# One launch of a two-stage graph network on 12,500 nodes and 200,000 edges: the first layer's edge stage joined with the count build, extra tiles one by one

## The chip, the core and the metric

The kernel runs on one NeuronCore of one Trainium2 chip. The core has five engines with queues of their own: TensorE (PE in the profile, its weight loads PEld), VectorE (DVE), ScalarE (ACT), GpSimd (POOL) and SyncE (SP). They share the on-chip memories and meet only at semaphores. The metric is the device time of one launch in microseconds (us); lower is better.

## What is computed

Three graph convolutions on the normalised input, and one message layer with edge features. Cut to what matters:

```python
loop = arange(N); s = concat([src, loop]); d = concat([dst, loop])      # every node also has itself
deg = segment_sum(1, d); dinv = rsqrt(deg)
norm = dinv[s] * dinv[d]
h = relu(layernorm(x))
for W, b in ((W1, b1), (W2, b2), (W3, b3)):                             # GCN layers 0, 1, 2
    h = segment_sum((h @ W)[s] * norm[:, None], d) + b                  # relu between layers
x = x + h
h = relu(layernorm(x))
filt = edge_attr_50 @ W_rad.T + b_rad
m = segment_sum((h @ W_pre.T + b_pre)[src] * filt, dst)
out = x + silu(m @ W_post.T + b_post)
```

There are 12,500 nodes with 64 features and 200,000 edges. The edges are sorted by destination `dst`, and the destinations are skewed: low nodes have many incoming edges, high nodes few. `src` is random. The dtype is float32.

## The kernel before

Nodes are cut into 98 windows of 128. Edges are cut into 196 blocks of 8 tiles of 128, and 4 blocks make a round. The first 50 windows of destinations (the head, 6400 nodes) are handled in another way than the rest (the tail):

- **Head, count build.** From the edges the kernel builds, once, the matrix of edge counts, source node by head destination. It goes by groups of 8 destinations: 800 groups, 16 to a window. For a group, DVE makes one one-hot of the source's row (`tile_hots`, L635) for its 2 main tiles of edges, and for each tile one one-hot of (source window, destination in the group), 784 wide (`joint_hot`, L859). PE multiplies them into PSUM (`joint_tile`, L1181, 2 matmuls of 392 columns a tile). A group whose edges lie in more than 2 tiles has extra tiles; they are made in sets of `EXTRA` = 2 tiles, two sets in flight. After two groups PE runs one closing matmul (L1215), and ACT turns the counts of both into fp8 in one go (L552). After a window, SP writes it to the HBM tensor `counts` (L396). The loop runs over 200 steps of 4 groups (`SETS`), and DVE may be 4 groups ahead of PE. DVE and PE read the tile numbers into registers at the start of a step (L887, L888, L1195).
- **Head, every GCN layer.** The counts of a window come back from HBM (L418), PE multiplies all 98 source windows of counts by the node features split in three bf16 parts (`dense_window`, L1098, 98 matmuls of 192 columns), and DVE adds the result to `node` (`take_dense`, L688, L692).
- **Tail, every GCN layer.** For 15 rounds of 4 blocks, POOL gathers the source rows of a block from the HBM tensor `table` (8 indirect DMAs, L500). DVE makes one-hots of the destinations (`one_hot`, L629) and splits the rows into three bf16 parts (`split_rows`, L646 to L653), PE multiplies (`product_split`, L1085, L1087), and DVE adds the sum to `sumT` (`add_sum`, L661). In a layer's edge pass a tail block and a head window take turns (`dense_turn`).

The order is written out by hand in one program for each engine: degrees, then the count build, then a layernorm (L601) and for each layer a projection (PE transposes and multiplies, DVE scales in L950 and writes the three parts in L960 to L966, SP writes `table`), the edge pass and a collection (L1000 to L1006). Within a projection's loop, DVE makes the parts of a group of 7 windows right behind that group's scaling. The number of rounds and of head windows comes from a check at the end of the build (`mode`, L929): if the counts do not add up to the degrees, every layer takes all edges as tail. For these inputs the counts add up. `gate` (L733) clears the head's sums where they are not wanted. The message layer takes all 196 blocks as tail, in float32, with edge filters.

## Time and profile before

| | us |
|---|---|
| median of 3 runs | 6310.55 |
| lowest and highest | 6275.51, 6314.47 |
| the profiled execution | 6314.64 |
| its span | 6312.8 |

| engine | busy us | share of the span |
|---|---|---|
| PE | 4668.7 | 74% |
| DVE | 3220.4 | 51% |
| POOL | 2908.4 | 46% |
| ACT | 856.6 | 14% |

Stages of the span, read from the times at which their lines first and last run: degrees and tables to 381 us, count build 381 to 1768, layernorm and projection 0 to 1886, edge pass 0 to 2539, collection 0 and projection 1 to 2668, edge pass 1 to 3303, the same again for layer 2 to 4068, collection, layernorm and projection to 4275, the message layer's edges to 6230, closing to 6312. An engine's busy share is an average over stages with different limits, so each stage is read by itself. Idle time in brackets stands before the instruction, with what ended it; "issue" means that the profile shows nothing that the engine waited for.

### The profile page before, as it was taken

Reading aid. Unit: us, or ns where it says so; the run is one execution under the profiler, and the core shown is the slowest. Engines: PE = TensorE matmul, PEld = TensorE weight load, DVE = VectorE, ACT = ScalarE, POOL = GpSimd, SP = SyncE. Lnnn points to the kernel's source line nnn. Section 1 sums busy time; section 2 is a strip of 40 time slices with the busy share of each in tenths; the row PEclk is TensorE's granted clock in tenths of the full one; section 3 lists DMA queues with packets and bytes.
Section 4 is the critical chain, followed back from the end, with each engine's and each line's share of the span. In section 5 each row is a group of like instructions: output and inputs, shape, how many; then the busy total and the mean of one; then the engine's idle time right before and its main releaser. Section 6 shows DMA issues by size and latency. Waiting matters only on the chain.

```text
span 6312.8 us, 113587 instructions
## 1 busy us (share of the span) xinstructions
PE 4668.7 (74%) x32080; PEld 3572.4 (57%) x32081; DVE 3220.4 (51%) x8761; ACT 856.6 (14%) x1382; POOL 2908.4 (46%) x3078
## 2 busy tenths in 40 slices
PE   6967676666659997799968999666666666666665
PEld 4732222222248885688847888455555555555555
DVE  6789998777764444644446444452222222222225
ACT  0002345555520000200001000010000000000002
POOL 0000000000007667177763766507777777777772
PEclk9999999999959997599976999656666666666665
DMA  1000011111114553155522555202222222222221
GB/s 32 0 0 41 41 61 61 71 71 71 71 60 160 167 168 94 53 172 167 174 65 82 167 170 173 64 24 47 46 47 47 47 46 47 47 46 47 47 46 34
DMA packets 165567, 484.92 MB, mean 77 GB/s; under 512 B 68364, under 2 KB 81740, under 8 KB 139924
## 3 DMA queue, kind: packets, MB, share of 16 engines
q1 hardware_dynamic: 69268, 385.60, 16.9%
q0 software_dynamic: 96256, 98.76, 8.3%
q8 instruction: 25, 0.41, 0.0%
q14 instruction: 18, 0.15, 0.0%
HBM read 387.82 MB, written 96.33 MB: 77 GB/s over the span
## 4 chain that ended last, share of the span: by engine, by line
PE 38%; POOL 25%; issue 16%; DVE 12%; DVEq 7%; DMA 1%; SPq 0%; POOLq 0%; ACT 0%; ACTq 0%
POOL rows_flat L500 25%; PE ps L1098 20%; DVE node L859 6%; PE ps L1155 5%; PE ps L1070 4%; PE ps L1087 4%; PE ps L1085 3%; DVE hot L635 2%; PE ps L1181 1%; DVEq L859 1%; DVEq L888 1%; PE ps L1056 1%; DVEq L887 1%; DVEq L635 1%; DVEq L903 1%
## 5 line engine op out<-in xcount | busy, mean ns | idle before, releaser
L500 POOL DMA_INDIRECT rows_flat<-table,row_stage x3008 | 2870.4, 954 | 1549.2 <-issue 1308.7
L1078 PE MATMUL ps<-hot,msg_flat 128*64 128x160 f32 x3136 | 807.9, 445 | 728.8 <-DVE msg_flat L722 728.8
L1181 PE MATMUL ps<-node,hot 128*128 128x392 f16 x4268 | 914.6, 342 | 489.6 <-DVE node L859 473.1
L1098 PE MATMUL ps<-wide,ring 128*128 128x192 bf16 x14700 | 1244.9, 247 | 0.0
L1098 PEld LDWEIGHTS ps<-wide,ring 128*128 128x128 fp8e4 x14700 | 1210.5, 98 | 13.0
L1078 PEld LDWEIGHTS ps<-hot,msg_flat 128*64 128x64 f32 x3136 | 649.9, 215 | 843.4 <-issue 711.4
L859 DVE TENSOR_SCALAR node<-rows_flat,wide 128x784 f16<-128x784 f16 x2134 | 928.8, 477 | 0.0
L1181 PEld LDWEIGHTS ps<-node,hot 128*128 128x128 f16 x4268 | 355.4, 100 | 940.2 <-issue 639.7
L484 POOL TENSOR_TENSOR found<-found,found_ring 128x8 f32<-128x8 f32 x50 | 24.7, 494 | 1698.9 <-ACT ring L552 1698.9
L629 DVE TENSOR_SCALAR hot<-iota,dst_rel 128x160 f32<-128x160 f32 (+1 forms) x3008 | 639.7, 291 | 265.2 <-issue 262.7
L552 ACT ACTIVATE ring<-ps 128x1568 fp8e4<-128x1568 f32 x400 | 590.8, 1477 | 763.6 <-PE ps L1215 763.3
L722 DVE TENSOR_TENSOR msg_flat<-rows_flat,ps 128x512 f32<-128x512 f32 x196 | 134.7, 687 | 1009.5 <-DMA rows_flat<-table,row_stage 1009.3
L565 ACT COPY row_stage<-row_i 128x8 int32 x376 | 74.0, 197 | 3741.7 <-DVE sumT L661 3737.6
L635 DVE TENSOR_TENSOR hot<-onehot_more,wide 128x256 f16<-128x256 f16 x1067 | 378.3, 355 | 229.9 <-issue 122.2
L1118 PEld LDWEIGHTS ps<-w_rad,ring 51*128 51x128 f32 x3136 | 431.0, 217 | 58.4 <-issue 58.4
L1118 PE MATMUL ps<-w_rad,ring 51*128 51x64 f32 x3136 | 459.8, 305 | 0.0
L688 DVE TENSOR_REDUCE dense_sum<-ps 128x64 f32<-128x192 f32 x150 | 53.7, 358 | 655.8 <-PE ps L1098 655.8
L661 DVE TENSOR_TENSOR sumT<-sumT,ps 64x160 f32 (+1 forms) x376 | 119.4, 318 | 486.0 <-issue 379.3
L1155 PE MATMUL ps<-hot 128*128 128x98 bf16 x1568 | 296.5, 360 | 50.5 <-DVE hot L635 50.5
L1155 PEld LDWEIGHTS ps<-hot 128*128 128x128 bf16 x1568 | 210.5, 147 | 135.7 <-issue 50.2
L1085 PE MATMUL ps<-hot 128*128 128x160 bf16 x720 | 182.6, 254 | 124.0 <-DVE hot L653 124.0
L635 DVE TENSOR_TENSOR hot<-onehot_more,ring 128x1024 bf16<-128x1024 bf16 (+1 forms) x392 | 229.0, 626 | 67.1 <-PE ps L1155 67.1
(146 smaller groups left out, 2945.6 us busy)
## 6 DMA issues: line engine op xcount, KB each, us to landing
ring<-counts SPq DMA_DIRECT2D x150, 1568.0 KB
counts<-ring SPq DMA_DIRECT2D x50, 1568.0 KB, 5.1
rows_flat<-table,row_stage POOLq DMA_INDIRECT x3008
ring<-in_radial SPq DMA_DIRECT2D x196, 200.0 KB
table<-node SPq DMA_DIRECT2D x56, 224.0 KB, 1.9
out<-node SPq DMA_DIRECT2D x13, 224.0 KB
ring<-in_dst SPq DMA_DIRECT2D x1, 784.0 KB
ring<-in_src SPq DMA_DIRECT2D x1, 784.0 KB
```

The lines of the kernel that those rows point to most:

```text
L500: nc.gpsimd.indirect_dma_start(out=rows[:, j, k * D:(k + 1) * D], out_offset=None, in_=table[:, :], in_offset=bass.IndirectOffsetOnAxis(ap ...
L552: nc.scalar.activation(to, of, ACT.Identity, scale=float(UNIT), saturate=True, accum_out=found_ring[:, h, t:t + 1]).then_inc(sub_copied, 1)
L629: one = nc.vector.tensor_scalar(to[:, k, :], columns, rel[:, bass.ds(tile0 + k, 1)], None, ALU.is_equal)
L635: return nc.vector.tensor_tensor(to, columns, of.unsqueeze(1).to_broadcast(to.shape), ALU.is_equal)
L859: return nc.vector.tensor_scalar(to, iota_joint, sub_start[:, bass.ds(sub, 1)], joint_of[:, bass.ds(t, 1)], ALU.add, ALU.is_equal)
L1070: z = nc.tensor.matmul(ps_z[:, h, i * D:(i + 1) * D], stage_fn[0:n, h, i * P:(i + 1) * P], w, start=True, stop=True)
L1078: s = nc.tensor.matmul(to, of, mats[:, k, :], start=(k == 0), stop=(k == BLOCK_TILES - 1))
L1085: nc.tensor.matmul(to, split_upper[j % 2][:, k, :], mat, start=(k == 0), stop=False, skip_group_check=True)
L1098: d = nc.tensor.matmul(ps_dense[:, h, :], count_ring[:, h, q, :], parts[:, q, :], start=(q == 0), stop=(q == WINDOWS - 1))
L1118: f = nc.tensor.matmul(ps_filt[:, j % 2, k * D:(k + 1) * D], radial_sb[:, j, k * P:(k + 1) * P], w_rad[:, :], start=True, stop=True)
L1155: d = nc.tensor.matmul(ps_deg, rem_hot[:, a, :, k], win_hot[:, a, :, k], start=(first and k == 0), stop=(last and k == BLOCK_TILES - 1))
L1181: m = nc.tensor.matmul(to[:, c, :], sources[:, :, k], joint[k][:, c * (JOINT // 2):(c + 1) * (JOINT // 2)], start=first, stop=True, skip_g ...
```

## The change

The first layer's layernorm, projection and table write now stand ahead of the count build. The build loop becomes `build_and_first_layer`: 25 iterations (pairs of windows) of 4 quarters. A quarter builds 8 groups (`subs` twice), then PE multiplies half a finished window of counts (`dense_part`, 49 matmuls, straight from the ring, without the way through HBM), and, in the first 15 iterations, a tail block is split, multiplied and added. Which rounds are tail is known before the build now (`tail_known`); the check comes afterwards, and if it fails the first layer is done again (`REDO`), which does not happen for these inputs. The counts are still written to HBM for layers 1 and 2.

With it come: `EXTRA` = 1, extra tiles made one by one in two buffers; the second main tile of a group is multiplied last, behind the extra tiles, and the closing matmul is gone; ACT converts one group at a time, 784 values instead of 1568, and the two PSUM buffers hold one group each instead of two; the found counts are added by DVE instead of POOL; POOL's gathers wait for `slot_free`; bases of tail blocks are clamped to the head's end and put back (`unclamp`) ahead of the message layer; the `gate` multiply is gone; and in every GCN projection the three bf16 parts are made in a second loop behind the whole first one (and behind clearing `sumT`), instead of within it.

The diff, cut to its core:

```diff
-EXTRA = 2
+EXTRA = 1
-        ps_count = [ps[:, 4 * a:4 * a + 4, 0:JOINT // 2] for a in range(2)]
+        ps_count = [ps[:, 4 + 2 * a:6 + 2 * a, 0:JOINT // 2] for a in range(2)]
@@ scalar
+            def evict(i, h, t):
+                act.wait_ge(main_used, i * (2 * TURNS) + (h * TURNS + t + 1 + SETS))
+                of = ps_count[t % 2].rearrange("p a (q d) -> p a q d", d=SUB)
+                nc.scalar.activation(to, of, ACT.Identity, scale=float(UNIT), saturate=True,
+                                     accum_out=found_ring[:, h, t:t + 1]).then_inc(sub_copied, 1)
@@ vector
-                dve.wait_ge(slot_free, at.turn(at.rounds, SLOTS))
-                nc.vector.tensor_scalar(sumT[:, 0:HEAD * P], sumT[:, 0:HEAD * P], gate[:, 0:1], None, ALU.mult)
+            def project(p):
+                with dve.Fori(0, GROUPS // 2) as g2:
+                    for h in range(2):
+                        ...
+                            nc.vector.tensor_tensor(mine, z, over_features(dinv[:, groups(g2 * 2 + h)]),
+                                                    ALU.mult).then_inc(z_used, 1)
+                if p:
+                    then(nc.vector.memset(sumT[:, :], 0.0))
+                settle()
+                if p < GCN_LAYERS:
+                    dve.wait_ge(z_used, (PROJECT(p) + 1) * GROUPS + 2)
+                    with dve.Fori(0, GROUPS) as g:
+                        ...
+                        nc.vector.tensor_copy(part[0], mine).then_inc(step, 1)
+                        nc.vector.tensor_tensor(tmp[:, :, :], mine, part[0], ALU.subtract).then_inc(step, 1)
+                        nc.vector.tensor_copy(part[1], tmp[:, :, :]).then_inc(step, 1)
+                        nc.vector.tensor_tensor(part[2], tmp[:, :, :], part[1], ALU.subtract).then_inc(step, 1)
+                    dve.drain().then_inc(parts_ready, 1)
+            def build_and_first_layer():
+                dve.wait_ge(table_written, 16 * GROUPS)
+                at = Pass(dve, FUSED)
+                with dve.Fori(0, PAIRS) as i:
+                    for j in range(SLOTS):
+                        h = j // 2
+                        with dve.Fori(0, P // SUB // SETS // 2) as q:
+                            subs(i * (2 * P // SUB // SETS) + j * (P // SUB // SETS // 2) + q)
+                        if j == 0:
+                            with dve.If(i > 0):
+                                take_dense(0, last, 0)
+                                keep_found(last, 1)
+                                with dve.If(last < at.rounds):
+                                    add_sum(at, last, SLOTS - 1, P)
+                        if j == 2:
+                            with dve.If(i > 0):
+                                take_dense(0, earlier(i), 1)
+                            keep_found(i, 0)
+                        with dve.If(i < at.rounds):
+                            split_block(at, i, j)
+                            if j:
+                                add_sum(at, i, j - 1, P)
+                            add_more(at, i, j, ps_more_fused[j % 2])
+            layernorm(2)
+            project(0)
+            build_and_first_layer()
@@ tensor
+            def dense_part(i, h, part):
+                if part == 0:
+                    pe.wait_ge(sub_copied, i * (2 * TURNS) + ((h + 1) * TURNS + 2))
+                    pe.wait_ge(dense_taken, i * 2 + (h + 1))
+                for q in range(part * (WINDOWS // 2), (part + 1) * (WINDOWS // 2)):
+                    d = nc.tensor.matmul(ps_dense[:, h, :], count_ring[:, h, q, :], parts[:, q, :],
+                                         start=(q == 0), stop=(q == WINDOWS - 1))
-                    if a % 2 == 0:
-                        pe.wait_ge(sub_copied, s4 * (SETS // 2) + (a // 2 + 1))
+                    pe.wait_ge(sub_copied, s4 * SETS + (a + 1))
-                    for k in range(MAIN):
-                        m = joint_tile(to, src_main[a], joint_main[a], k, k == 0)
-                    m.then_inc(main_used, 1)
+                    for k in range(MAIN - 1):
+                        joint_tile(to, src_main[a], joint_main[a], k, k == 0)
                     ...
-                    if a % 2:
-                        nc.tensor.matmul(to[:, 1, 0:1], zeros16[:, :], zeros16[:, 0:1],
-                                         start=False, stop=True, skip_group_check=True).then_inc(built, 1)
+                    joint_tile(to, src_main[a], joint_main[a], MAIN - 1, False).then_inc(main_used, 1)
+            def build_and_first_layer():
+                with pe.Fori(0, PAIRS) as i:
+                    for j in range(SLOTS):
+                        with pe.Fori(0, P // SUB // SETS // 2) as q:
+                            subs(i * (2 * P // SUB // SETS) + j * (P // SUB // SETS // 2) + q)
+                        if j < 2:
+                            with pe.If(i > 0):
+                                dense_part(earlier(i), 1, j)
+                        else:
+                            dense_part(i, 0, j - 2)
+                        with pe.If(i < at.rounds):
+                            split_block(at, i, j, ps_more_fused[j % 2])
```

Two places in the order of the instructions. In the first, a GCN layer's projection on DVE before: each group's scaling (L950, from PSUM into `node`) is followed by the instructions that write its parts into `wide`.

```order
L950 TENSOR_TENSOR node<-ps,dinv 128x448
L960 ISA
L960 REGISTER_ALU
L960 COPY wide<-node 128x7x64
```

And the same place in the change (layer 0), where L998 is the scaling, and L1009 the head of the second loop, which holds the four instructions on the parts (L1017 to L1023).

```order
L998 TENSOR_TENSOR node<-ps,dinv 128x448
L993 REGISTER_ALU
L993 COMPARE_AND_BRANCH
L1009 UNCONDITIONAL_BRANCH
L1009 ISA
L1017 ISA
L1017 REGISTER_ALU
L1017 COPY wide<-node 128x7x64
```

The parts have moved behind the end of the scaling loop. The second place is PE at the end of a step of 4 groups. Before, the group's matmuls (`node` holds the joint one-hots, `hot` those of the source) end with the closing matmul, and the next thing is the loop's own branch:

```order
L1181 MATMUL ps<-node,hot 128x392 x4
L1190 REGISTER_ALU
L1211 UNCONDITIONAL_BRANCH
L1215 MATMUL ps<-zeros 128x1
L1194 REGISTER_ALU
L1194 COMPARE_AND_BRANCH
```

In the change (`sumT` and `stage_fn` hold the one-hots now), after the extra tile's two matmuls the second main tile's two follow, then the inner loop's branch (L1390), half a window of counts (L1354) and the tail block (L1238, L1240, repeated 8 times):

```order
L1343 MATMUL ps<-sumT,stage_fn 128x392 x2
L1364 REGISTER_ALU
L1382 UNCONDITIONAL_BRANCH
L1343 MATMUL ps<-sumT,stage_fn 128x392 x2
L1390 REGISTER_ALU
L1390 COMPARE_AND_BRANCH
L1393 COMPARE_AND_BRANCH
L1350 ISA
L1351 ISA
L1354 MATMUL ps<-wide,ring 128x192 x49
L1393 UNCONDITIONAL_BRANCH
L1397 COMPARE_AND_BRANCH
```

So the work of the first layer's edge pass now stands in PE's queue between groups of the build. In the built program the outer loop of the build is 826 instructions long on DVE; the longest loop on DVE before is 286. On PE it is 1241, against 1057 before.

## Rows read from the trace of the kernel before

**Rows 1.** Busy time by stage; columns are named in the first line.

```profile
core 0: us, PE busy (x) PEld busy (x) DVE busy (x) ACT busy (x) POOL busy (x), PEclk, DMA share, GB/s
381.00:1768.00 1387.00, 923.85 (x4668) 395.35 (x4666) 1155.39 (x3197) 626.71 (x800) 24.52 (x49) 0.97 0.14 57
1768.00:1886.00 118.00, 67.01 (x294) 57.63 (x294) 83.41 (x114) 20.48 (x34) 0.66 (x3) 0.50 0.11 41
1886.00:2539.00 653.00, 593.14 (x5860) 501.95 (x5860) 269.41 (x881) 11.05 (x56) 459.29 (x480) 0.92 0.46 147
```

**Rows 2.** Timeline of DVE in the build: start, length, instruction, idle before.

```profile
1352.62 0.29 DVE L635 TENSOR_TENSOR hot<-onehot_more,wide 128x256 f16<-128x256 f16 x1 [0.94 <-issue]
...
1358.00 0.29 DVE L635 TENSOR_TENSOR hot<-onehot_more,wide 128x256 f16<-128x256 f16 x1 [1.05 <-PE ps L1181]
```

**Rows 3.** Timeline of DVE in the build, behind a window's write.

```profile
1387.27 0.43 DVE L635 TENSOR_TENSOR hot<-onehot_more,wide 128x256 f16<-128x256 f16 x1 [2.36 <-issue]
```

**Rows 4.** Timeline of DVE in the build, extra sets of one group.

```profile
390.93 0.29 DVE L635 TENSOR_TENSOR hot<-onehot_more,wide 128x256 f16<-128x256 f16 x1 [0.17 <-issue]
...
393.17 0.29 DVE L635 TENSOR_TENSOR hot<-onehot_more,wide 128x256 f16<-128x256 f16 x1 [0.18 <-issue]
```

**Rows 5.** Timeline of PE's weight loads in the build, two groups.

```profile
1354.95 0.46 PEld L1181 LDWEIGHTS ps<-node,hot 128*128 128x128 f16 x4 [0.68 <-issue]
...
1355.94 0.46 PEld L1181 LDWEIGHTS ps<-node,hot 128*128 128x128 f16 x4 [0.20 <-issue]
```

**Rows 6.** Timeline of ACT in the build, one conversion of two groups.

```profile
1352.80 1.48 ACT L552 ACTIVATE ring<-ps 128x1568 fp8e4<-128x1568 f32 x1 [0.54 <-PE ps L1215]
1354.18 0.19 ACT L552 ACTIVATION_READ_ACCUMULATOR ring<-ps 128x1 f32 x1
```

**Rows 7.** Timeline of edge pass 0, one turn on DVE, then PE's window of counts.

```profile
2004.93 1.49 DVE L629 TENSOR_SCALAR hot<-iota,dst_rel 128x160 bf16<-128x160 bf16 x8 [0.76 <-issue]
...
2007.98 0.69 DVE L653 TENSOR_TENSOR hot<-hot 128x512 bf16<-128x512 f32 x1
2013.26 0.36 DVE L688 TENSOR_REDUCE dense_sum<-ps 128x64 f32<-128x192 f32 x1 [4.58 <-PE ps L1098]
2013.78 0.23 DVE L692 SCALAR_TENSOR_TENSOR node<-dense_sum,node 128x64 f32 x1 [0.17 <-DVE dense_sum L688]
2014.79 0.32 DVE L661 TENSOR_TENSOR sumT<-sumT,ps 128x160 f32 x1 [0.78 <-issue]
2015.87 0.80 DVE L629 TENSOR_SCALAR hot<-iota,dst_rel 128x160 bf16<-128x160 bf16 x4 [0.76 <-issue]
2004.96 8.26 PE L1098 MATMUL ps<-wide,ring 128*128 128x192 bf16 x98
```

**Rows 8.** Groups of instructions, the page's and edge pass 0's: count | busy, mean.

```profile
L859 DVE TENSOR_SCALAR node<-rows_flat,wide 128x784 f16<-128x784 f16 x2134 | 928.8, 477 | 0.0
L500 POOL DMA_INDIRECT rows_flat<-table,row_stage x480 | 459.3, 957 | 292.3 <-issue 256.1 <-ACT row_stage L565 36.2
```

**Rows 9.** Timeline of DVE at the end of projections 0 and 1.

```profile
1882.10 0.62 DVE L950 TENSOR_TENSOR node<-ps,dinv 128x448 f32 x1
...
2641.14 0.62 DVE L950 TENSOR_TENSOR node<-ps,dinv 128x448 f32 x1
2641.98 0.62 DVE L960 CAST wide<-node  x1 [0.23 <-DVE node L950]
...
2644.17 0.62 DVE L966 TENSOR_TENSOR wide<-tmp,wide 128x448 f32 x1
2647.39 10.64 DVE L971 MEMSET sumT<- 128x12704 f32 x1 [2.60 <-issue]
```

**Rows 10.** Timeline of DVE at the end of edge pass 0.

```profile
2538.77 3.55 DVE L733 TENSOR_SCALAR sumT<-sumT,gate 128x6400 f32<-128x6400 f32 x1 [0.86 <-DVE sumT L661]
```

**Rows 11.** The page's DMA queues: packets, MB, share of 16 engines.

```profile
q8 instruction: 25, 0.41, 0.0%
q14 instruction: 18, 0.15, 0.0%
```

511 lines of the change are left out of this document (317 added, 194 removed).

## Prediction

> **What bounds the kernel now.** I read first the busy time by stage [rows 1]. The build takes 1387 us and edge pass 0 takes 653. In the build DVE is busy for 1155 us and PE for 924; in the edge pass PE is busy for 593 and DVE for only 269. The two stages lean on different engines, so joining them looks promising. The question is what is left of it when the idle time of DVE in the build turns out not to be free.
>
> The timeline of DVE in the build answers that. A step of 4 groups without extra tiles takes 1358.00 - 1352.62 = 5.38 us [rows 2], steadily, step after step. The idle 0.94 to 1.05 us ahead of it is the reading of two sets of registers and the loop's branch. The second row puts it down to PE, but the length of a step does not change with that label, and PE's groups wait a little for DVE (the 0.20 and 0.68 us in [rows 5]): I read it as DVE's own queue. So 200 x 5.38 = 1076 us of the build are DVE's, idle time included. Once per window, when its counts go out to HBM, a step is longer: DVE idles 2.36 us where otherwise it idles about 1 [rows 3], so some 1.2 us a window, 60 in all. The rest, 1387 - 1076 - 60 = 251 us, are the extra sets: the page counts 2134 one-hots of 784, 1600 are those of the main tiles, so 267 sets of two tiles [rows 8]. That is 0.94 us a set; in a long run of them two sets take 393.17 - 390.93 = 2.24 us [rows 4], 1.12 a set.
>
> PE is not far behind. From one group to the next where it hardly waits it takes 1355.94 - 1354.95 = 0.99 us [rows 5], though its matmuls are four; the rest is its queue's branches. In the edge pass a turn (a tail block and a window of counts) takes 2015.87 - 2004.93 = 10.94 us, of which the window is 8.26, all on PE [rows 7].
>
> **The build loop after the change, by quarters.** A quarter is two steps, half a window of counts and, in 60 of the 100 quarters, a tail block.
>
> DVE, in a quarter with a block: two steps, 10.76. The long read, 1.2 for two quarters, 0.6. One-hots and split from 2004.93 to 2008.67, 3.74 us; from the end of the counts' addition (2014.01) to the next one-hot (2015.87) lie 1.86 us with the block's own addition and its register reads [rows 7]; together 5.6. Taking a window, 0.36 + 0.23 and the gap between, 0.75 for two quarters, 0.4. Adding the found counts, two more conditions and an inner loop's start: about 0.6, an estimate from the 0.76 us that such reads and branches leave idle [rows 7]. Sum 18.0.
>
> PE, in the same quarter: the matmuls of 8 groups at 0.99 would be 7.9, plus the loop's end and read twice, about 1 us each as on DVE, so 9.9. But now the second main tile comes behind both branches, one PSUM buffer holds one group, and group n+2 may start only when ACT has converted group n. ACT's conversion of two groups is 1.48 + 0.19 [rows 6]; that of one lies between half of the first, 0.74, plus 0.19, and the whole. I take 1.0. A group of about 1.2 us from its first weight load to its last matmul, its conversion, and two hand-overs of about 0.1 make 2.4 us for two groups, 1.2 a group: 8 groups in 9.7 to 10.7, I take 10.4. Half a window is 4.1, a block's products are what is left of the turn, 10.94 - 8.26 = 2.7, conditions 0.3 [rows 7]. Sum 17.5. DVE may be 4 groups ahead, and while it splits a block PE multiplies counts, so the two overlap: the quarter is the longer sum and a little, 18.2 us. 60 of them: 1092.
>
> Without a block DVE needs 18.0 - 5.6 = 12.4 and PE 17.5 - 2.7 = 14.8: PE sets the pace, 15.0 us. 40 of them: 600.
>
> Extra tiles: by the input's destinations there are 388 one by one, where there were 267 sets. Each costs between half a set, 0.47, and a whole one, 0.94; its one-hots are half of a set's, its waits and registers a whole set's. I take 0.64, 250 us, so that edit alone is worth nothing against 251: fewer one-hots (1988 for 2134) and more turns. The last window's products stand behind the loop, 8.3. The joined loop is then 1092 + 600 + 250 + 8 = **1950 us**. From both sides: with 17.3 and 13.8 a quarter and 0.5 a tile it is 1792; with 19.8, 16.8 and 0.9 it is 2217.
>
> **The hidden part: gathers.** POOL gathers a block in 8 instructions that are 0.957 us each [rows 8], with about 0.3 between them. That is some 10 us, and a block has a quarter of 18 us; a block's slot is free three quarters ahead. So the gathers lie under DVE's work, and would up to 1.8 times their length. Here DVE was 269 of 653 us busy [rows 1]; in the loop it is busy nearly always. The Trainium skill, page "SBUF — State Buffer", section on the shared port pair, says that DVE in its fast two-port modes locks GpSimd out of it, and that descriptors of GpSimd's own DMAs wait. That speaks against joining the gathers with DVE's busiest stage. With the rows' cover of 1.8 times it changes no term of mine.
>
> **What moves around it.** Before, layernorm and projection 0 end with the last scaling at 1882.10 + 0.62 [rows 9], 115 us behind the build's end; they stand ahead of the build now at the same price. But the parts follow in a loop of their own. One group's parts run from 2641.98 to 2644.17 + 0.62, 2.8 us [rows 9], 3.1 with the loop: 14 groups are 43 us in which PE waits for `parts_ready`, where before only the last group's 3 us stood there. For layer 0 that is 44 us (it covers the table's write and the first gathers). For layers 1 and 2 the parts come behind the 10.64 us of clearing, and the edge pass, bound by PE's windows, starts 40 us later each: +80. The cover that is gone is PE's time in the projection, which took 118 us with the layernorm for 67 of PE [rows 1]. The `gate` multiply goes, -3.6 in each of layers 1 and 2 [rows 10]. Clearing half of `sumT` before the build, -5. `unclamp`, about ten short DVE instructions, lies under the message layer's first gathers. The check after the loop, register reads and the empty `REDO` cost about what the old pass took to its collection: +1.
>
> **The sum.** Before, from the build's start at 381 to the last addition of edge pass 0 at 2538: 2157. After: -5 + 115 + 44 + 1950 + 1 = 2105, so -52. With +80 and -7 the change comes to **+21 us**. The profiled execution's span is 6312.8 (6314.6 with what lies around it) and the median 6310.55, 4 below: 6310.55 + 21 = 6332, I say **6335 us**.
>
> **The rivals.**
> 1. *The engines overlap better.* PE's groups run at 1.0 us and without blocks DVE sets the pace: quarters of 17.5 and 13 us, extra tiles at 0.55. The loop is 1050 + 520 + 213 + 8 = 1791, less than mine by 159. Halfway there, 1850, it gives 6235. For it speaks the 0.99 us of [rows 5]; against it that group n+2 waits for ACT. It decides below 1.05 us a group.
> 2. *A new wait: the conversion of single groups* (the one on the other side). One group in flight in each buffer ties PE to ACT and to itself. At 1.5 us a group, quarters are 20.2 with a block and 17.4 without: 1212 + 696 + 250 + 8 = 2166, +216, about 6550; at 1.35, 6440. ACT's 1.48 us for two groups speaks against the full price, and that PE's queue passes two branches in each group speaks for it. It decides above about 1.3.
> 3. *Code.* DVE's loop body is 826 instructions in the built program, three times its longest before; the page counts 25 and 18 code packets for the whole run [rows 11], so no loop before reads its code again. If this one does, and DVE waits as in the longest unexplained gap before a stage, 2.6 us [rows 9], once an iteration, it costs 15 x 2.6 = 39 us in the iterations with blocks; at each of five branches back, 195. Time 6375 to 6530. The Trainium skill, page "Runtime: NRT & Kernel Launch", section "Instruction fetch mechanics", has this as a rule: the instruction memory of an engine other than PE holds 512 instructions, and a taken branch out of it waits for a fetch. By that rule DVE's loop does not fit and all loops before do; what a wait costs here no row shows.
> 4. *It doesn't do what it says.* The first layer's work only lengthens each quarter, because PE's blocks come late every time: 10.8 + 4.1 + 2.7 + 3.7 = 21 us; loop 2100, 6485.
>
> **Chances.** Forecast 0.45 (own range 6270 to 6400); rival 1 0.20; rival 2 0.18; rival 3 0.12; rival 4 0.05. The range 6235 to 6480 leaves out the far end of rivals 1, 2 and 3. About 1%, 63 us, is what a measurement of this kernel can tell from no change. Below 6247 lies most of rival 1 and nothing else: 0.19. Above 6374 lie most of rivals 2 and 3, rival 4 and a tenth of the forecast: 0.36. The rest, 0.45, is within 1%.
>
> **What would show it.** In the profile after: in layers 1 and 2 the first product of counts stands 40 us further behind the last scaling than now; the loop from its first one-hot to the last window takes 1950 us; a quarter with a block takes 18 us and DVE is busy in it without waits for PE; one without takes 15 and DVE's one-hots of the source wait for PE's L1343; GpSimd is never named as what DVE waits for. DVE gaps of over 2 us at the outer loop's head, with many more code packets, would be rival 3. A busy ACT between PE's groups would be rival 2. Quarters far below 17 us, or a half clock in the loop (the granted clock is 0.97 in the build and 0.92 in the edge pass [rows 1], near the full 2.4 GHz), would prove my sum wrong.

## The result and the profile after

Over 20 timed runs of each, the changed kernel takes 6267.17 us (median, 6235.64 to 6323.17) and the kernel before 6314.46 (6275.51 to 6328.37). The ratio is 0.994, with a 95% interval of 0.9921 to 0.9959. So the change makes the kernel faster by 0.6%, surely but by less than 1%: the medians lie 47 us apart, the means 39. The forecast was 21 us slower. The measured time lies inside the stated range (6235 to 6480), but the change went the other way.

From the page of the profiled execution after (6264.8 us): the span, busy times, the code queues, and the two groups of one-hots of the joined loop.

```profile
span 6263.0 us, 114127 instructions
PE 4667.6 (75%) x31388; PEld 3424.1 (55%) x31389; DVE 3181.7 (51%) x8799; ACT 951.1 (15%) x2182; POOL 2930.3 (47%) x3027
q14 instruction: 217, 1.78, 0.1%
q8 instruction: 26, 0.43, 0.0%
L961 DVE TENSOR_SCALAR sumT<-stage_fn,sub_start,sumT 128x784 f16<-128x784 f16 x1988 | 891.5, 481 | 0.0
L508 POOL DMA_INDIRECT rows_flat<-table,row_stage x3008 | 2917.2, 970 | 2136.9 <-issue 1844.2
```

The busy times of PE, DVE and POOL hardly move; ACT's grows by 94 us. What moves besides is the idle time, and one queue: 217 packets of code, where [rows 11] has 18.

Busy time by stage after: layernorm and projection 0, parts 0, the joined loop (with blocks, and its last part without), projection 1 with its parts, edge pass 1, the scaling loop of projection 3.

```profile
core 0: us, PE busy (x) PEld busy (x) DVE busy (x) ACT busy (x) POOL busy (x), PEclk, DMA share, GB/s
372.00:485.00 113.00, 67.01 (x294) 57.64 (x294) 47.79 (x49) 20.15 (x33) 0.39 (x1) 0.50 0.07 27
485.00:531.00 46.00, 0.00 (x0) 0.00 (x0) 34.85 (x56) 0.00 (x0) 35.46 (x30) 0.50 0.12 24
531.00:1900.00 1369.00, 1085.76 (x6412) 521.13 (x6413) 1019.75 (x3055) 437.09 (x1003) 459.35 (x452) 0.91 0.14 46
1900.00:2480.00 580.00, 475.47 (x3426) 265.37 (x3425) 378.46 (x1055) 295.46 (x654) 0.41 (x1) 1.00 0.14 59
2533.00:2626.00 93.00, 32.68 (x267) 29.44 (x266) 54.24 (x71) 16.32 (x26) 35.65 (x32) 0.67 0.24 80
2626.00:3265.00 639.00, 591.66 (x5857) 501.14 (x5857) 268.82 (x879) 11.05 (x56) 429.12 (x448) 0.93 0.45 144
4158.00:4190.00 32.00, 32.00 (x265) 28.89 (x262) 7.95 (x13) 16.29 (x26) 0.00 (x0) 1.00 0.22 86
```

The two executions can be laid side by side at five marks (trace of before, trace of after, difference):

| from | to | before us | after us | difference |
|---|---|---|---|---|
| start | first scaling of projection 1 | 2590.2 | 2533.3 | -56.9 |
| first scaling 1 | first one-hot of edge pass 1 | 70.3 | 93.0 | +22.7 |
| edge pass 1 | first scaling 2 | 693.9 | 689.2 | -4.7 |
| first scaling 2 | first one-hot of edge pass 2 | 70.6 | 92.8 | +22.2 |
| edge pass 2 | first scaling 3 | 754.9 | 749.5 | -5.4 |
| first scaling 3 | first message one-hot | 75.7 | 52.7 | -23.0 |
| message layer | end | 2057.2 | 2052.5 | -4.7 |

The sum is -49.8, the difference of the spans. The joined loop, from its first one-hot at 531 to its last window's take at 2479, took 1948 us; 1950 was forecast. The reader is to see three things that the forecast did not have. The parts cost +22.7 and +22.2 where +40 was forecast. Projection 3, whose scaling loop was not changed, became 23 us shorter. And the joined loop is right as a sum of wrong terms, as the experiments show.

### The profile page after: what moved, and what is told of

Same layout as the page of the kernel before. It is cut to its first block, busy times and chain, and to the rows that moved or that the text cites. A ratio compares the mean times of both kernels' runs of the same rounds, so it can differ in the third digit from the quotient of the medians.

```text
span 6263.0 us, 114127 instructions
## 1 busy us (share of the span) xinstructions
PE 4667.6 (75%) x31388; PEld 3424.1 (55%) x31389; DVE 3181.7 (51%) x8799; ACT 951.1 (15%) x2182; POOL 2930.3 (47%) x3027
## 3 DMA queue, kind: packets, MB, share of 16 engines
q14 instruction: 217, 1.78, 0.1%
## 4 chain that ended last, share of the span: by engine, by line
PE 36%; POOL 25%; issue 18%; DVE 13%; DVEq 7%; DMA 1%; ACT 0%; SPq 0%; POOLq 0%; ACTq 0%
POOL rows_flat L508 25%; PE ps L1251 13%; PE ps L1343 5%; PE ps L1317 5%; PE ps L1223 4%; DVE sumT L961 4%; PE ps L1354 3%; PE ps L1240 3%; PE ps L1238 2%; DVE stage_fn L689 1%; PE ps L1209 1%; DVE hot L683 1%; DVEq L689 1%; DVEq L712 1%; DVE hot L1189 1%
## 5 line engine op out<-in xcount | busy, mean ns | idle before, releaser
L508 POOL DMA_INDIRECT rows_flat<-table,row_stage x3008 | 2917.2, 970 | 2136.9 <-issue 1844.2
L1343 PE MATMUL ps<-sumT,stage_fn 128*128 128x392 f16 x3976 | 980.4, 358 | 418.1 <-DVE sumT L961 234.4
L961 DVE TENSOR_SCALAR sumT<-stage_fn,sub_start,sumT 128x784 f16<-128x784 f16 x1988 | 891.5, 481 | 0.0
L1343 PEld LDWEIGHTS ps<-sumT,stage_fn 128*128 128x128 f16 x3976 | 287.8, 101 | 1086.6 <-issue 829.4
L585 ACT ACTIVATE ring<-ps 128x784 fp8e4<-128x784 f32 x800 | 658.5, 823 | 1255.5 <-PE ps L1343 1250.0
L689 DVE TENSOR_TENSOR stage_fn<-stage_fn,src_rem 128x256 f16<-128x256 f16 (+1 forms) x1188 | 393.7, 331 | 481.8 <-issue 289.4
L1354 PE MATMUL ps<-wide,ring 128*128 128x192 bf16 x4900 | 420.2, 246 | 6.0 <-ACT ring L585 3.6
L1354 PEld LDWEIGHTS ps<-wide,ring 128*128 128x128 fp8e4 x4900 | 402.3, 98 | 32.2 <-issue 28.2
L1238 PE MATMUL ps<-hot 128*128 128x160 bf16 x720 | 180.4, 251 | 173.9 <-DVE hot L707 173.8
```

Of the source, the lines that this page charges most:

```text
L508: nc.gpsimd.indirect_dma_start(out=rows[:, j, k * D:(k + 1) * D], out_offset=None, in_=table[:, :], in_offset=bass.IndirectOffsetOnAxis(ap ...
L585: nc.scalar.activation(to, of, ACT.Identity, scale=float(UNIT), saturate=True, accum_out=found_ring[:, h, t:t + 1]).then_inc(sub_copied, 1)
L689: return nc.vector.tensor_tensor(to, columns, of.unsqueeze(1).to_broadcast(to.shape), ALU.is_equal)
L961: return nc.vector.tensor_scalar(to, iota_joint, sub_start[:, bass.ds(sub, 1)], joint_of[:, bass.ds(t, 1)], ALU.add, ALU.is_equal)
L1238: nc.tensor.matmul(to, split_upper[j % 2][:, k, :], mat, start=(k == 0), stop=False, skip_group_check=True)
L1343: m = nc.tensor.matmul(to[:, c, :], sources[:, :, k], joint[k][:, c * (JOINT // 2):(c + 1) * (JOINT // 2)], start=first, stop=True, skip_g ...
```

## Experiment 1: is DVE's loop fetched again, and what does that cost?

DVE shows an idle stretch at the head of each iteration of the joined loop. Its timeline after, at two heads, 55.5 us apart:

```profile
2025.73 0.42 DVE L689 TENSOR_TENSOR stage_fn<-stage_fn,src_rem 128x256 f16<-128x256 f16 x1 [5.09 <-issue]
2081.27 0.29 DVE L689 TENSOR_TENSOR stage_fn<-stage_fn,src_rem 128x256 f16<-128x256 f16 x1 [5.35 <-issue]
```

A usual step has about 1 us there [rows 2]. In the trace's records the branch back (L1057) and the next instruction are 3.33 us apart in the median (2.73 to 3.91), 24 times, 80 us in all. Six kernels with loops of different length are compared. The cuts, in short (the first goes into all but the one with 554 instructions; the last into those with 554, 446 and 326):

```
-  If n > 1: Fori(0, n >> 1): extra tile in buffer 0, extra tile in buffer 1
-  If n & 1: extra tile in buffer 0
+  If n > 0: Fori(0, n): extra tile in the buffer that a register names (turn & 1)
...
-  add_more(at, i, j, ...)        # in the joined loop, on DVE, and more_products on PE
...
-  before each slot j:    Fori(0, 2) as q: subs(...)
+  before slots 0 and 2:  Fori(0, 4) as q: subs(...)
```

The lengths are those of DVE's loop body in the built program. The second cut leaves out the code for blocks that span more than 160 nodes, which these inputs never enter (510 and 326). A block's eight destination columns are also copied to a fixed place first, in the four kernels with the first cut.

> The kernel after with DVE's joined loop shortened from 826 to 630 instructions: one copy of an extra tile's code in place of three (its buffer chosen by a register), and a block's eight destination columns copied to a fixed place first. Same sums. Theory (the loop's code is fetched again at each branch back as long as it is too long): the gap of 3.4 us ahead of the first work of each iteration stays, an iteration without a block and without extra tiles stays at 55.3 us, code packets stay near 217. Rival (the gap is the loop's own branch and register reads, or grows with the length): it shrinks in the proportion 630 to 826, to 2.6 us, 54.5 us an iteration. An extra tile gets dearer by up to 0.2 us through the registers, so the whole loop is 1930 to 2030 us.

> As the kernel of 630 instructions, and without the code for spans of over 160 nodes in the joined loop on DVE and PE (these inputs never enter it): 510 instructions. Theory: the loop fits, the gap of 3.4 us at each of the 25 iterations falls under 1 us, an iteration without a block goes from 55.3 to about 52, code packets fall from 217 to near 18, and the whole is 85 us (1.4%) faster than with 630, of which some 5 are the skipped conditions. Rival (the gap has nothing to do with length): the gap stays at 3.4 us and the whole moves by under 10 us.

> The kernel after with one edit: the steps of the count build stand twice in the joined loop instead of four times (four steps in a row ahead of slots 0 and 2, none ahead of 1 and 3). DVE's loop body falls from 826 to 554 instructions. From the runs so far: with bodies of 630 and 510 the gap at the branch back was still 3.3 us an iteration and 7 and 6 packets of code came for each. Theory (the loop must fit whole, with what is fetched ahead of need): at 554 the gap is still 3.3 us, packets near 6 an iteration. The mixing gets coarser, PE has no groups while DVE makes two blocks' operands: if that costs, an iteration with blocks goes from 74 to 78 or more; if DVE's own work is all that counts there, it stays at 74.

> The kernel of 510 instructions with the same edit, the count build's steps twice in place of four times: 326 instructions, near the 282 and 286 of the loops that fetched nothing. Theory: code packets fall from 167 to about 18 for the whole run, the gap ahead of an iteration falls from 3.3 us to under 0.5, an iteration without a block goes from 49.0 to 46, and the loop is 24 x 3 = 70 us shorter than with 510, less what the coarser mixing costs (0 to 4 us an iteration with blocks). Rival (the gap is the price of a loop of any length around inner loops): gap and packets stay.

> The kernel of 326 instructions with the code for wide spans left in (never entered): 446 instructions. If what counts is that the loop is below 512, it is not fetched again: packets near 22, gap under 0.5 us. If room for code fetched ahead is needed too (510 did not fit), 446 may not fit: 5 packets and a gap of 3.3 us an iteration, loop 80 us longer than with 326 instead of about 10.

Measured, with ratios to the kernel before (6314.5 to 6316.7 us); the gaps are the 24 between the branch back and the next instruction:

| DVE's loop | median us | ratio, 95% | joined one-hots, first to last, us | packets | gap, median us | the first 15 gaps in sum, us |
|---|---|---|---|---|---|---|
| 826 (after) | 6267.2 | 0.994, 0.9921 to 0.9959 | 1931.4 | 217 | 3.33 | 49.2 |
| 630 | 6239.9 | 0.987, 0.9844 to 0.9896 | 1919.7 | 192 | 3.44 | 54.5 |
| 554 | 6391.3 | 1.011, 1.0054 to 1.0166 | 1920.0 | 237 | 2.92 | 42.1 |
| 510 | 6177.6 | 0.9782, 0.9766 to 0.9798 | 1845.4 | 167 | 3.93 | 63.9 |
| 446 | 6261.1 | 0.9913, 0.9886 to 0.9939 | 1866.1 | 143 | 2.94 | 42.4 |
| 326 | 6115.8 | 0.968, 0.9654 to 0.9706 | 1779.9 | 22 | 0.25 | 3.9 |

The rows behind the last line, from the page with 326 instructions and from its view of the joined one-hots' line (count, ns min/median/max, first and last start):

```profile
q14 instruction: 22, 0.18, 0.0%
...
L977 DVE TENSOR_SCALAR sumT<-stage_fn,sub_start,sumT x1988: 464/477/701, 502.0 to 2281.9; 128x784 f16<-128x784 f16 x157, 128x784 f16 x42
```

And the same two of the kernel with 446:

```profile
q14 instruction: 143, 1.16, 0.1%
...
L977 DVE TENSOR_SCALAR sumT<-stage_fn,sub_start,sumT x1988: 465/477/697, 501.7 to 2367.8; 128x784 f16<-128x784 f16 x157, 128x784 f16 x42
```

The fetching is shown: packets come 5 to 8 an iteration in every kernel from 446 instructions up, and none comes with 326, where the gap goes from 3 us or more to 0.25. At the head of an iteration the kernel with 326 has DVE waiting for PE and no longer for its own queue:

```profile
1936.11 0.29 DVE L696 TENSOR_TENSOR stage_fn<-stage_fn,src_rem 128x256 f16<-128x256 f16 x1 [2.07 <-PE ps L1354]
```

My expectation of 510 was wrong: it did not fit, and 446 does not either. Two more were missed. With 630, an iteration without blocks takes 49.1 us where I expected 55.3 again, at an unchanged gap: the shorter code for extra tiles is worth 6 us an iteration there, and that isn't fetching. With 326 it takes 49.8 where I expected 46. The Trainium skill, page "Runtime: NRT & Kernel Launch", section "Instruction fetch mechanics", gives the memory as 512 instructions in two halves, of which the code ahead is read while the present one runs. The trace agrees with the halves more than with the sum: 326 fits, 446 doesn't. I had used only the sum of this rule. An estimate from that page's figures: with halves of 256, a loop of 446 lies in two of them only if it begins in the first 66 places of one, and the place of a loop would decide as much as its length. No run here moves a loop and nothing else, so this is not shown.

The kernel with 554 instructions shows that length alone isn't the rule. Its median is 1% above the kernel before, while its joined loop is no longer than with 630. The time goes mostly in edge pass 2 (and 28 us in projection 3, at half clock in this trace), whose code is the same as in edge pass 1 (282 instructions on DVE) but lies elsewhere in the program. Edge passes 1 and 2 of this kernel:

```profile
2620.00:3248.00 628.00, 587.48 (x5837) 499.99 (x5837) 265.58 (x871) 11.06 (x56) 425.08 (x445) 0.94 0.45 146
3406.00:4118.00 712.00, 622.29 (x5838) 520.20 (x5838) 268.06 (x872) 11.05 (x56) 423.24 (x445) 0.88 0.40 130
```

and DVE in the second, at two places of an iteration:

```profile
3658.07 0.26 DVE L683 TENSOR_SCALAR hot<-iota,dst_rel 128x160 bf16<-128x160 bf16 x1 [5.26 <-issue]
3660.08 1.38 DVE L683 TENSOR_SCALAR hot<-iota,dst_rel 128x160 bf16<-128x160 bf16 x7 [1.75 <-issue]
```

Where edge pass 1 has 0.75 there, pass 2 waits 5.26 and 1.75 us, in all its 14 returns, and 72 of the 237 packets of code come in this pass, where the kernel after has 2. This costs 86 us in a pass that PE bounds otherwise. So where a loop lies decides as well; which places are bad I did not find out.

How much of the gain from 826 to 326 is the fetching can be bounded only. From 510 to 326 the loop loses 65.5 us. The gaps behind the 15 iterations with blocks are longer than elsewhere with 510, 63.9 us in sum against 3.9 with 326, so 60 us of idle time vanish there; but the steps also stand four in a row now, and what that is worth by itself no run shows. In the iterations without blocks the gap was hidden: 49.0 us with 510, 49.8 with 326, where DVE waits 3.1 and 3.3 us for PE instead. If the edits simply added, the fetch would be worth as little as 12 us (65.5 less the 53.6 that the same coarser mixing gave from 630 to 446). So it is 12 to 65 us. The never-entered code for wide spans costs more than the 5 us that I had expected: its register reads and branches on DVE and PE make 1919.7 - 1845.4 = 74 us from 630 to 510, 1.2 us for each of 60 blocks, and this although the gaps grew (63.9 us for 54.5).

## Experiment 2: what do the parts cost?

```
 def project(p):   # layers 1 and 2
     Fori(0, GROUPS // 2): scale a group
+        wait for it; its four part operations
-    Fori(0, GROUPS): the four part operations of a group
```

> The kernel after with the parts of layers 1 and 2 made inside the scaling loop, as before the change; layer 0 stays as it is. By the prediction's step (PE's 67 us of projection hide them, the separate loop costs 40 each): 80 us faster than after, near 6187. By what the trace after suggests (the scaling loop itself fell from 51 to 33 us when the parts left it, so that the separate loop costs 43 - 18): 45 to 50 us faster, near 6218. Rival: the faster message layer of after hangs on this too, and the gain shrinks to 20 to 30.

> The kernel before with only this part of the change: in all three layers the parts are made in a loop of their own behind the scaling. By the prediction's step 3 x 40 = 120 us slower than before, 6430; by the trace after 3 x 25 = 75 slower, 6388, with scaling loops of 33 us instead of 51 in layers 1 and 2. The message layer should not move; if it gets 24 us faster, as in after, the separate loop does that through the clock.

Measured: 6251.4 us (0.9896, 0.9879 to 0.9912) for the parts back inside, 16 us below after; and 6403.4 us (1.0148, 1.0117 to 1.0178) for the kernel before with a loop apart, 88 above before. The first gains less than I expected under any case, the second lies between my two numbers, and the clock has a part in both. The views by stretch of the scaling loops say how. After, projections 0 and 1:

```profile
423.00:484.00 61.00, 60.73 (x267) 52.26 (x266) 8.21 (x14) 16.07 (x26) 0.00 (x0) 0.50 0.13 49
2533.00:2566.00 33.00, 32.68 (x267) 29.44 (x266) 8.19 (x14) 16.32 (x26) 0.00 (x0) 0.99 0.22 84
```

The same 267 matmuls take 60.7 us at a granted clock of 0.50 (1.2 GHz) and 32.7 at 0.99 (2.4 GHz). Before, projection 1 in two halves, with parts inside, and projection 3:

```profile
2590.00:2616.00 26.00, 24.52 (x159) 21.51 (x159) 21.84 (x36) 10.65 (x16) 0.00 (x0) 0.78 0.16 62
2616.00:2641.00 25.00, 24.34 (x108) 21.35 (x108) 17.76 (x29) 5.67 (x11) 0.00 (x0) 0.50 0.15 56
4180.00:4241.00 61.00, 61.00 (x270) 52.75 (x269) 8.44 (x14) 16.30 (x26) 0.00 (x0) 0.50 0.13 49
```

With the parts inside, DVE is busy for 21.84 of 26 us, PE does 159 of its 267 matmuls in them, and the clock falls to 0.50 within the loop: 51 us in sum. Without them it stays where it begins. With the parts back inside after, projections 1 and 2:

```profile
2539.00:2601.00 62.00, 60.79 (x267) 52.27 (x266) 40.81 (x66) 16.32 (x26) 0.00 (x0) 0.50 0.13 48
3311.00:3337.00 26.00, 24.53 (x160) 21.55 (x160) 21.82 (x36) 10.59 (x16) 0.00 (x0) 0.79 0.16 62
```

From the first scaling to the first one-hot of the edge pass the traces give: inside 70 to 72 us where the clock began full and 81.3 where it was half; apart 92 to 95 where full, and 120 to 121 where half (projection 2 of the kernel before with a loop apart, projection 1 of the one with 510 instructions). So the move costs 22.7 us at full clock, and 120.8 - 81.3 = 39.5 at half. My +40 was the price at half clock.

Why, then, is the kernel with parts inside no more than 16 us below after? Projection 3 took the gain back. Its scaling loop ran at full clock after (4158 to 4190 in the stages above). In the kernel after with parts inside, and in the kernel before with a loop apart:

```profile
4133.00:4194.00 61.00, 61.00 (x269) 52.75 (x269) 8.37 (x14) 16.30 (x26) 0.00 (x0) 0.50 0.13 49
```

```profile
4253.00:4286.00 33.00, 33.00 (x271) 29.90 (x269) 8.45 (x14) 16.29 (x26) 0.00 (x0) 0.99 0.23 87
```

The other traces go the same way. Three pairs differ in nothing but the place of the parts of these layers (or of all three): the kernel before and the same with a loop apart, after and the same with parts inside, that with 326 instructions and the same with parts inside (experiment 6). Each pair turns this way, by one trace on each side. Of the kernels without added matmuls (experiment 5), those whose parts of layers 1 and 2 stand apart ran projection 3 at full clock in 9 of 10 traces (all but the one with the loop of 554); those with the parts inside ran it at half clock in 5 of 5, the kernel before among them. 45 us less for the parts and 28 more for projection 3 make 17 us less, which is what the medians show. The rival that I wrote down, that the faster end of after hangs on the parts too, had this right. Why the clock of projection 3 goes with them stays open.

## Experiment 3: one extra tile or two at a time?

```
-EXTRA = 1          # after       |   -EXTRA = 2          # before
+EXTRA = 2                        |   +EXTRA = 1
```

> The kernel after with EXTRA = 2 as before the change: 267 sets of two extra tiles for 388 single ones, all else the same. By the prediction this edit is worth nothing (251 for 250 us). Both take one pair of branches and waits, a set has one more one-hot of 0.48 us: if a single tile costs 0.64 and a set 0.94, the loop is 1948 us, give or take 10. Rival: here DVE's cost of a turn is mostly its one-hots, so a single costs 0.5 and a set 1.1: the loop is 100 us longer with sets.

> The kernel before with EXTRA = 1 alone: 388 single extra tiles for 267 sets of two in the separate build. By the prediction 0 (250 for 251 us). With sets in the joined loop that loop was 45 us longer, so by the same price: the build 45 us shorter than in the kernel before, near 6270. Then the joining itself, with its fetched code, brings about nothing.

Measured: 6313.2 us (1.0004, 0.9986 to 1.0021) for after with sets of two, 46 above after; 6338.6 us (1.0035, 1.0011 to 1.0059) for before with single tiles, 23 above before. Both are against what I expected, and with opposite signs. The one-hots' lines of the kernel after with sets, and of the kernel before with singles:

```profile
L961 DVE TENSOR_SCALAR sumT<-stage_fn,sub_start,sumT x2134: 464/477/707, 502.0 to 2478.3; 128x784 f16<-128x784 f16 x194
```

```profile
L859 DVE TENSOR_SCALAR node<-rows_flat,wide x1988: 468/477/483, 378.5 to 1787.4; 128x784 f16<-128x784 f16 x199
```

The joined loop is 1976.3 us with sets and 1931.4 with singles: 45 us. The separate build is 1408.9 with singles, and 1385.2 in the kernel before: 24 us the other way. Part of the cause is in long runs of extra tiles. DVE in the kernel before with singles:

```profile
389.18 0.29 DVE L635 TENSOR_TENSOR hot<-onehot_more,wide 128x128 f16<-128x128 f16 x1 [0.48 <-PE ps L1181]
...
391.01 0.29 DVE L635 TENSOR_TENSOR hot<-onehot_more,wide 128x128 f16<-128x128 f16 x1 [0.48 <-PE ps L1181]
```

and after:

```profile
564.21 0.29 DVE L689 TENSOR_TENSOR stage_fn<-stage_fn,src_rem 128x128 f16<-128x128 f16 x1 [0.21 <-PE ps L1343]
...
565.71 0.29 DVE L689 TENSOR_TENSOR stage_fn<-stage_fn,src_rem 128x128 f16<-128x128 f16 x1 [0.21 <-PE ps L1343]
```

In a run a single tile costs 1.83 / 2 = 0.91 us in the separate build, 1.50 / 2 = 0.75 in the joined loop, and a tile in a set 1.12 / 2 = 0.56 [rows 4]. So the first pair of windows, with 38 extra tiles in one group, loses by singles (197.9 for 157.4 us in the separate build, 220.7 for 189.6 in the joined loop), and the later ones, where most groups that have any have one, gain. That the gain is the larger in the joined loop has a second cause, which is the code of experiment 1: with sets the loop brings 242 packets of code, 9 an iteration for 8, and its gaps at the branch back add up to 101.5 us for 79.8. So up to 22 of the 45 us are a price of the longer code, and not of how the tiles are paired. The joining with sets gives nothing at all (1.0004): the gain of the change hangs on the pairing of the two edits.

## Experiment 4: does PE set the pace without blocks?

```
-for q in range(part * (WINDOWS // 2), (part + 1) * (WINDOWS // 2)):
+for q in (range(0, WINDOWS // 4) if part == 0 else range(WINDOWS - WINDOWS // 4, WINDOWS)):
```

> The kernel after, leaving out half of the first layer's products of counts (each of the four parts in an iteration multiplies 24 or 25 windows in place of 49), which takes 2.1 us of PE's time from each quarter and nothing from DVE's. If PE sets the pace of the iterations without blocks, as the prediction had it, these fall from 55.3 to 47 us; if DVE does, they stay. Between the two if it is now one and now the other: quarters 2 and 3 (15.1 and 16.0 us) would fall and 0 and 1 (12.7 and 11.5) stay. In the iterations with blocks, where DVE sets the pace, 74 us stay.

Measured: 6256.3 us (0.9903, 0.9869 to 0.9937). The joined one-hots' line:

```profile
L961 DVE TENSOR_SCALAR sumT<-stage_fn,sub_start,sumT x1988: 464/477/708, 531.4 to 2457.4; 128x784 f16<-128x784 f16 x199
```

The loop lost 5.4 us. An iteration without blocks went from 55.3 to 53.3 us, one with blocks from 74.3 to 74.7. PE's busy time in an iteration without blocks fell from 45.2 to 39.5 us and not by the full 8, since its clock fell too (0.94 for 1.00). Without blocks the two quarters that I had expected to fall did, by 1.7 and 1.4 us (15.1 to 13.4, 16.0 to 14.6), and quarter 0 grew by 1.4. DVE's waits from 2000 to 2300 us, in the kernel after and in this one:

```profile
DVE stage_fn L689 <- PE ps L1343: 63.7, 42, 3.6
DVE stage_fn L689 <- issue: 36.0, 11, 5.3
```

```profile
DVE stage_fn L689 <- issue: 47.9, 15, 6.4
DVE stage_fn L689 <- PE ps L1343: 45.2, 33, 2.2
```

So PE's sum alone does not set the pace without blocks: of 8 us taken from it 2 came back. But DVE alone does not either, for it waits 11.7 us for PE in each of these iterations, as the prediction had said. With blocks PE's counts are worth nothing.

## Experiment 5: the clock of the projections

```
+    Fori(0, n): 8 matmuls 128x128 by 128x256 bf16, result unread   # ahead of projections 0 and 3
```

> The kernel after with matmuls whose result nobody reads put ahead of projection 0 and of projection 3, where PE waits for the layernorm (25 turns of 8 matmuls of 128x256 bf16, 20 us at full clock, 43 at half); the results stay. In the traces so far a plain scaling loop takes either 32.7 us (granted clock 1.00) or 60.8 (0.50), never between. Theory: it is PE's state as the loop begins, so work just ahead of it makes both 32.7 each time: 28 us less where after is at half clock (projection 0 in its trace), and the spread of the timed runs (6235 to 6323 in after) narrows. Rival: the clock does not follow what PE did just before; both lengths go on turning up, and the median stays.

> The kernel after with the unread matmuls reaching up to the projections this time (64 turns ahead of projection 0, 40 ahead of 3; at full clock 0.92 us a turn). The shorter ones ended at 375 us, 40 ahead of projection 0, and the clock was at 0.50 again from 395. Theory (the state as the loop begins): projections 0 and 3 take 32.7 us each; in the timed runs the slowest clusters (6298 and 6323) thin out, median 6240 to 6265. Rival (the clock does not follow it): projection 0 still takes 60.8 in the trace, median 6267 to 6300.

> The kernel after once more, unchanged, for a second trace. Its 20 timed runs stand in clusters at 6236, 6266, 6298 and 6323. Theory: each of the four projections takes 32.7 or 60.8 us by the clock, and the cluster is the number at half clock (0, 1, 2, 3); the first trace had one, at 6265. This trace's time must be 6236 plus 28 to 30 for each projection of 60.8. Rival: the clusters come from elsewhere (gathers, the message layer), and the projections of this trace don't answer to its time.

Measured: 6296.7 us (0.9958, 0.9928 to 0.9989) with the short ones, 6309.5 us (0.9974, 0.9944 to 1.0004) with the long, 6265.3 us for after once more. The long ones, at projection 0:

```profile
395.00:410.00 15.00, 15.00 (x140) 13.45 (x138) 12.17 (x20) 0.29 (x1) 0.00 (x0) 1.00 0.00 0
410.00:423.00 13.00, 7.03 (x36) 5.88 (x34) 6.01 (x1) 3.79 (x6) 0.00 (x0) 0.67 0.01 1
423.00:484.00 61.00, 60.84 (x267) 52.27 (x266) 8.12 (x13) 16.07 (x26) 0.00 (x0) 0.50 0.13 49
```

PE was busy at full clock until 410, 13 us ahead of the scaling loop, and the loop still ran at 0.50, 60.6 us. So my theory fell: work that far ahead does not make the loop run at full clock. The medians are 30 and 42 us above after, but the intervals of the ratios overlap with after's, so harm isn't shown. What decides the clock stays open.

The second trace of after bears on the spread. In all traces the plain scaling loops are 32.6 to 33.1 or 60.6 to 60.8 us, and the spans of after and of the two kernels with unread matmuls follow their number: one slow loop in both traces of after (6263.0 and 6262.9), two with the short extra matmuls (6300.7), three with the long (6326.8). The 20 timed runs of after stand at 6236 to 6239 (4 runs), 6265 to 6272 (9), 6297 to 6299 (6) and 6323 (1), in steps of about 29, so by this count 1.2 slow loops a run. Both traces fell on the second step and have projection 0 as the slow one; the other steps were never traced for this kernel, so the count fits them and isn't shown. In the second trace of after the clock's column does not show it:

```profile
423.00:484.00 61.00, 61.00 (x268) 52.52 (x267) 8.12 (x13) 16.07 (x26) 0.00 (x0) 1.00 0.13 49
2532.00:2565.00 33.00, 32.76 (x268) 29.44 (x267) 8.12 (x13) 16.31 (x26) 0.00 (x0) 1.00 0.22 83
```

The same matmuls, 61 against 33 us, with 1.00 in both rows. The first 1.00 is no reading: this trace has no record of the clock before 547.6 us (the first one has its first at 353.7), and the column shows 1.00 where there is none. The length of known work is the better clock.

## Experiment 6: the better version

> The kernel with 326 instructions in DVE's joined loop (6116 us) and the parts of all three layers made inside the scaling loops, as before the change. From the traces: from the first scaling to the first one-hot of layers 1 and 2 it is 93.0 us with a separate loop and 70.3 with the parts inside where the clock allows, so 2 x 23; in layer 0, 25 to 39: 6035 to 6060, if no loop is newly fetched by its place in the program.

> As the last one, with layer 0's parts still in a loop of their own: 2 x 23 us faster than the kernel of 326 instructions, 6070. If the clock falls in these projections once DVE's parts slow them, a scaling loop is 61 in place of 51 us and the gain 2 x 11, 6094.

> The kernel with 326 instructions and all parts inside (6046 us), with the long unread matmuls ahead of projections 0 and 3. If they set the clock: projection 0, with the parts inside, 51 for 61 us, projection 3 32.7 for 60.8, so 6046 - 10 - 14 = 6020, and a narrower spread than 6017 to 6061. If not: 6046, or some us more.

Measured: 6046.2 us (0.9558, 0.9527 to 0.9588) with the loop of 326 instructions and all parts inside the scaling loops; 6094.3 us (0.9644, 0.9607 to 0.968) with layer 0's apart; 6043.4 us (0.957, 0.9534 to 0.9606) with the unread matmuls in addition, which bring nothing. The first is 4.4% faster than the kernel before and beats both: its median is 269 us lower, where the change as made has 47. The second hit my 6094, but by luck: I had reckoned with scaling loops of 61 us in layers 1 and 2. They took 50 and 52 in its trace, and it was projection 3 that went to half clock, 61 for 33, as in experiment 2.

The first kernel keeps the joining and the single tiles, fits DVE's loop, and gives back the separate loop of parts. It leaves out, in the joined loop, the code for spans of over 160 nodes, so for other inputs it would need that code in a branch outside the loop.

## Why the prediction was wrong

- **The joined loop, 1950 us: right as a sum, wrong in its terms.** A quarter with a block was 18.2 and is 74.3 / 4 = 18.6 us, with 0.8 of fetched code in it. A quarter without was 15.0, paced by PE, and is 55.3 / 4 = 13.8: the step that PE's sum sets the pace there failed (experiment 4: 2.1 us less for PE in a quarter make 0.5). With 60 and 40 quarters that is 1114 and 553; the extra tiles are the rest, 1948 - 1114 - 553 - 8 = 273 us, 0.70 each where I took 0.64. Errors of +22, -47 and +23 cancel.
- **"That edit alone is worth nothing": wrong.** I gave each kernel one price for a tile. In the joined loop singles save 45 us against sets, up to 22 of them by shorter waits for code; in the separate build they lose 24.
- **Parts, +80 for layers 1 and 2: the step that failed, a mis-sized term, and the reason for the wrong sign.** It measured +44.9. I took PE's time in the projection as fixed, from projection 0, which runs at a granted clock of 0.50 [rows 1], and so all of DVE's 40 us as lost. But in layers 1 and 2 the scaling loop had been 51 us, its clock falling on the way; without the parts it is 33. Measured right, this term alone turns +21 into -14. At half clock throughout, +39.5, my number would have been right.
- **Projection 3, a term put at nothing: -23 us.** Its scaling loop ran at full clock after and at half before (33 for 61 us). By the count in experiment 2 this comes with the parts standing apart, in 9 of 10 traces against none of 5, so it is most likely a part of what the change does, and not the chance of one execution. The mechanism is not shown.
- **Rival 3, code: it came, at 3.33 us a branch back and 80 us of gaps in all**, 49 of them in the iterations with blocks, and the price of 2.6 was near. I gave it 0.12 as a case of its own, when it was a term that stood beside the others. It is in the 18.6 and 13.8 above.
- **Rival 1, better overlap:** it came half, in the quarters without blocks (halfway to its loop would have been 1870 us, not the 1850 that I wrote). **Rival 2, the conversion of single groups:** ACT is named for 3.3 us of PE's waits in 148 us with blocks and for 15.8 in 300 without; it did not come at the price that I gave it. **Rival 4:** no.
- **Right:** gathers stay hidden (970 ns for 957, and GpSimd never named as what DVE waits for in the loop); the gate's 3.6 us (4.7 and 5.4 with all else in the edge passes); layernorm, projection and parts 0 ahead of the loop; the whole stretch up to projection 1, -57 for -52.

The sum with the measured terms is -57 + 45 - 15 (the gate, and small things that I can't explain) = -27, and projection 3 makes it -50 in this trace. The timed runs show -47 by their medians and -39 by their means. That the time still lay in my range is luck in part: the loop's 1950 is a sum of errors that cancel.

## What to carry to other kernels

Before a loop is made longer by joining two stages, count its instructions on the engine that sets the pace: here a DVE body of 326 ran without fetching and 446 did not, at 3 us or more for each branch back, and the same loop of 282, which stands twice in one program, was fetched in one place and not in the other. When work moves out of a loop, price the loop that stays as well as the new one: what slowed it is gone, and PE's clock may change with it, there and in a later stage that nobody touched. And price an edit inside the kernel that it will stand in: the same constant was worth -45 us in one and +24 in the other, in part through the length of the code.

## What the runs showed of the hardware that I had not expected

- A DVE loop of 446 to 826 instructions brought 5 to 8 packets of code of 8 KB at each iteration (1.78 MB for 217; 9 with sets of two extra tiles) and held DVE for 2.7 to 5.3 us at the branch back (medians 2.92 to 3.93). With 326: none, 0.25 us. A loop of 282 instructions in one place in one kernel brought about 5 an iteration and 5.26 us of waiting, 86 us in the pass.
- The same 14 groups of a projection took 32.7 or 60.7 us, all at one clock or all at the other, now this projection and now that one in kernels that don't differ there, and PE kept fully busy at 1.00 until 13 us before did not prevent 0.50. The runs of one kernel spread over 88 us in steps of about 29, which fits none to three slow loops; one slow loop at the second step is what two traces show.
- The clock of projection 3 went with where the parts of layers 1 and 2 are made, a whole edge pass ahead of it and more: full in 9 of 10 traces with the parts apart, half in 5 of 5 with them inside.
- The column of the granted clock read 1.00 in a stretch whose matmuls ran at half speed, because the trace has no clock record there.
- Reading a register from memory and branching past code that is never entered, on two engines, came to 1.2 us a block, 74 us in the loop.
